# Weights times values and the output product of a masked cross-attention: float32 in 32-column tiles in place of split halves in full width

## The reference, cut to what matters

```python
q, k, v = norm(x) @ Wq.T, ctx @ Wk.T, ctx @ Wv.T       # heads of 32 columns
s = q[b, h] @ k[b, h].T / sqrt(32) + mask              # 128 x 2048
p = exp(s - max(s))
o[b, h] = (p @ v[b, h]) / sum(p)                       # 128 x 32
x[b] = x[b] + concat_h(o[b, h]) @ Wo.T                 # 128 x 512
```

## Time and profile before

| | |
|---|---|
| median of 3 runs | 1824.59 us (1823.38 to 1826.69) |
| profiled execution | 1827.8 us, its span 1826.4 us |
| TensorE, VectorE, ScalarE, GpSimd busy | 95%, 64%, 54%, 13% |
| mean granted TensorE clock | 0.983 |

### The profile page before, as it was taken

The page is one execution under the profiler, slowest core; times in us unless marked ns, Lnnn a source line. Parts: engine busy times, 40 slices in busy tenths (PEclk is TensorE's granted clock), DMA queues, the critical chain, the costliest instruction groups (busy, mean ns, idle before and its releaser), DMA issues.

```text
span 1826.4 us, 26578 instructions
## 1 busy us (share of the span) xinstructions
PE 1742.8 (95%) x9474; PEld 1429.8 (78%) x9474; DVE 1172.3 (64%) x2457; ACT 984.8 (54%) x2037; POOL 236.8 (13%) x138
## 2 busy tenths in 40 slices
PE   8999999999999999999999999999899879999998
PEld 5778888877888789999899888887455557778787
DVE  5777777765544246667677767998534356775755
ACT  6676666652443135565566656887322345665653
POOL 0000000000000031112111312232101012221222
PEclk9999999999999999999999999999999879999999
DMA  6322322217501698778677767677500347786721
GB/s 229 120 104 81 104 81 94 81 59 293 173 1 65 210 306 252 238 233 239 191 238 232 237 198 206 183 196 234 200 6 7 127 150 258 244 308 199 274 69 62
DMA packets 146848, 309.53 MB, mean 169 GB/s; under 512 B 11440, under 2 KB 100784, under 8 KB 135152
## 3 DMA queue, kind: packets, MB, share of 16 engines
q1 hardware_dynamic: 144784, 301.32, 50.9%
q0 software_dynamic: 1920, 6.36, 1.1%
HBM read 226.88 MB, written 80.76 MB: 168 GB/s over the span
## 4 chain that ended last, share of the span: by engine, by line
PE 78%; DVE 10%; ACT 4%; issue 3%; DMA 2%; DVEq 1%; SPq 1%; POOL 0%; ACTq 0%; POOLq 0%
PE bank L128 13%; PE bank L130 13%; PE bank L129 13%; PE bank L1298 4%; PE bank L2219 4%; PE bank L2220 4%; PE bank L2223 4%; PE bank L1694 4%; PE bank L1321 2%; PE bank L1322 2%; PE bank L1288 2%; DVE PTL L1428 2%; DVE TT L1417 2%; PE bank L1787 2%; ACT T L1837 1%
## 5 line engine op out<-in xcount | busy, mean ns | idle before, releaser
L1372 ACT CAST PTH<-bank 128x512 fp32r<-128x512 f32 x256 | 149.9, 586 | 166.2 <-PE bank L1298 166.2
L1428 DVE TENSOR_TENSOR PTL<-bank,PTH 128x512 fp32r<-128x512 f32 x256 | 176.0, 687 | 94.6 <-ACT PTH L1372 93.6
L2520 DVE TENSOR_TENSOR WS<-EW,WS 128x1024 fp32r<-128x1024 f32 (+1 forms) x120 | 148.3, 1243 | 83.0 <-ACT WS L2358 80.8
L1365 ACT ACTIVATE TT<-TT,MX 128x512 f32<-128x512 f32 x256 | 186.5, 729 | 8.5 <-DVE MX L1423 8.5
L1417 DVE CUSTOM_DVE_ANT_0 TT<-bank,MASK 128x512 f32<-128x512 f32 x256 | 174.2, 682 | 2.1 <-PE bank L1288 1.9
L2358 ACT CAST WS<-EW 128x1024 fp32r<-128x1024 f32 (+1 forms) x144 | 139.2, 978 | 64.5 <-PE bank L2223 63.7
L1298 PE MATMUL bank<-IDN,TT 128*128 128x128 f32 x1024 | 155.2, 274 | 4.1 <-DVE PTL L1428 3.7
L128 PE MATMUL bank<-BCH,WKT 128*128 128x256 f32 x512 | 148.2, 289 | 4.5 <-DVE BCL L355 4.5
L129 PE MATMUL bank<-BCL,WKT 128*128 128x256 f32 x512 | 144.8, 283 | 0.0
L130 PE MATMUL bank<-BCH,WKT 128*128 128x256 f32 x512 | 144.8, 283 | 0.0
L1321 PE MATMUL bank<-PTH,VG 128*128 128x256 f32 x512 | 142.6, 300 | 0.2 <-DVE PTL L1428 0.2
(11 more groups left out here) (320 smaller groups left out, 4365.3 us busy)
## 6 DMA issues: line engine op xcount, KB each, us to landing
EW<-in_ewg SPq DMA_DIRECT2D x48, 1024.0 KB, 5.6
KST<-tmp_k SPq DMA_DIRECT2D x43, 768.0 KB, 5.8
tmp_k<-EKH SPq DMA_DIRECT2D x128, 256.0 KB, 2.8
EW<-in_ewg SPq DMA_DIRECT2D x24, 768.0 KB, 4.6
CT<-in_ctxT SPq DMA_DIRECT2D x32, 512.0 KB, 3.2
CN<-in_ctxN SPq DMA_DIRECT2D x32, 512.0 KB, 3.2
BCT<-in_ctxT SPq DMA_DIRECT2D x32, 512.0 KB, 3.6
tmp_k<-EKL SPq DMA_DIRECT2D x64, 256.0 KB, 2.8
```

The lines of the kernel that those rows point to most:

```text
L1365: act.activation(TT[:, n % 4, cs], TT[:, n % 4, cs], ACT.Exp, bias=MX[:, n % 4, 5:6], scale=SC1, accum_out=SUM[:, b % 2, h, kc:kc + 1]).th ...
L1372: act.copy(PTH[:, g % NP], bank[turn_bank[g]][:]).then_inc(*p_high.up)
L1428: dve.tensor_tensor(PTL[:, q], bank[turn_bank[g]][:], f(PTH[:, q]), ALU.subtract).then_inc(*p_low.up)
```

## The change

The values stay as they are loaded, in float32, 64 columns for a pair, straight into VG; GpSimd's split is gone, and SyncE itself waits until a buffer of VG is free. The turned weights are kept in float32 in one tile PT: ScalarE copies the banks of even steps, VectorE those of odd steps. `value` now does four float32 products, each with 32 stationary columns (one head) by 128 moving ones. The two heads of a pair write 32 bank rows each, at rows 0 and 32 for even pairs, 64 and 96 for odd pairs. The reciprocals are spread by two products of the same shape, with 32 columns of ONES. OTS then has 128 distinct rows for two pairs (a "quad" of heads), the output product takes 4 tiles for a batch instead of 8, and VectorE does one multiplication for a pair instead of two. The core of the diff:

```diff
 
         WT = Region(g_at)
-        WO1 = WT("WO1", [128, 8, 512])
+        WO1 = WT("WO1", [128, 4, 512])
...
-        VG = A("VG", [128, 2, 16, 128], F32R)
+        VG = A("VG", [128, 2, 16, 64])
         at_t = A.at
-        VR = A("VR", [128, 1024])
         TT = A("TT", [128, 4, 2048])
         al = Region(at_t)
         QH = al("QH", [128, 4, 512], F32R)
         QL = al("QL", [128, 4, 512], F32R)
         NP = 4
-        PTH = A("PTH", [128, NP, 512], F32R)
-        PTL = A("PTL", [128, NP, 512], F32R)
+        PT = A("PT", [128, NP, 512])
         assert A.at <= g_at
         A = Region(wq_at)
         MASK = A("MASK", [128, 2, 2048], BF16)
         MUI = YT[:, 3, :].bitcast(I32)
         MU = YT[:, 3, :].bitcast(U8)
-        OTS = YT[:, 0:2, :].rearrange("p a (c q) -> p (a c) q", c=4)
-        LR = YT[:, 2, 0:256].rearrange("p (a q) -> p a q", a=2)
+        OTS = YT[:, 0, :].rearrange("p (c q) -> p c q", c=4)
         DG = YT[:, 2, 256:512].rearrange("p (a q) -> p a q", a=2)
         MX = A("MX", [128, 4, 8])
         SUM = A("SUM", [128, 2, 16, 4])
...
                     return None
-                if waiting[0][0] % 8 == 0 and left <= 0:
+                if waiting[0][0] % 4 == 0 and left <= 0:
                     out_bank = 2
                 if out_bank is None:
-                    if len(waiting) < 8:
+                    if len(waiting) < 4:
                         return None
-                    bk, n = 5 + turns % 2, 8
+                    bk, n = 5 + turns % 2, 4
                     turns += 1
                 else:
...
                         value_bank[v // 8] = 7 if left > 0 or v // 8 % 2 else 3
-                    if v % 8 == 7:
-                        waiting.append((v // 8, v))
+                    if v % 16 == 15:
+                        waiting.append((v // 16, v))
...
-        sums_mm, wo_mm = S.new("pe", 32), S.new("pe", 32)
-        s_exp, p_high, o_kept = S.new("act", 256), S.new("act", 256), S.new("act", 32)
+        sums_mm, wo_mm = S.new("pe", 32), S.new("pe", 16)
+        s_exp, p_act, o_kept = S.new("act", 256), S.new("act", 128), S.new("act", 32)
         cross_root = S.new("act", 3)
-        s_masked, s_max, p_low = S.new("dve", 256), S.new("dve", 64), S.new("dve", 256)
+        s_masked, s_max, p_dve = S.new("dve", 256), S.new("dve", 64), S.new("dve", 128)
         sums_diag, o_scaled, x_added, cross_var = S.new("dve", 32), S.new("dve", 32), S.new("dve", 4), S.new("dve", 3)
-        vg_high, vg_low, mask_made = S.new("pool", 32), S.new("pool", 32), S.new("pool", 4)
-        ld_qs, ld_vr, ld_mask = [S.keep("ld", 16) for _ in range(2)], S.keep("ld", 16), S.keep("ld", 16)
+        mask_made = S.new("pool", 4)
+        ld_qs, ld_vg = ([S.keep("ld", 16) for _ in range(2)] for _ in range(2))
+        ld_mask = S.keep("ld", 16)
...
+        def p_kept(g):
+
+            return (p_dve if g % 2 else p_act)[g // 2]
+
+        def rows_of(p):
+
+            return 64 * (p % 2)
+
         def cross_pe(bg, bg2):
-            emptied = {3: ev_act[31], 2: ev_dve[31]}
+            emptied = {3: ev_act[31], 2: ev_dve[31], (3, 0): ev_act[31], (3, 1): ev_act[31]}
 
             def score(g):
                 n, kc = g // 4, g % 4
@@ -1297,40 +1303,39 @@
                     kt, n = 2 * pc + j // 2, 2 * p + j % 2
                     m = pe.transpose(bank[bk][:, 128 * j:128 * j + 128], TT[:, n % 4, 128 * kt:128 * kt + 128], IDN[:])
                 m.then_inc(*t_mm.up)
-                emptied[bk] = p_low[g]
+                emptied[bk] = p_kept(g)
 
             def value(g):
                 p, pc, q = g // 8, g % 8, g % NP
-                vb = value_bank[p]
-                pe.wait_ge(*p_low[g])
+                vb, half = value_bank[p], (value_bank[p], p % 2)
+                heads = [slice(rows_of(p) + 32 * h, rows_of(p) + 32 * h + 32) for h in range(2)]
+                pe.wait_ge(*p_kept(g))
                 if pc == 0:
-                    pe.wait_ge(*vg_low[p])
-                    if vb in emptied:
-                        pe.wait_ge(*emptied[vb])
-                    emptied[vb] = o_scaled[p]
+                    pe.wait_ge(*ld_vg[p % 2][p // 2])
+                    if half in emptied:
+                        pe.wait_ge(*emptied[half])
+                    emptied[half] = o_scaled[p]
                     pe.wait_ge(*sums_diag[p])
-                    if p == 0:
-                        pe.wait_ge(*ld_lr[0])
                     for h in range(2):
-                        m = pe.matmul(bank[vb][:, 256:384], LR[:, h, :], DG[:, h, :], start=(h == 0), stop=(h == 1))
+                        m = pe.matmul(bank[vb][heads[h], 256:384], ONES[:, 0:32], DG[:, h, :], start=True, stop=True)
...
                     m.then_inc(*sums_mm.up)
                 for j in range(2):
                     kt = 2 * pc + j
-                    v = VG[:, p % 2, kt, :]
-                    js = slice(256 * j, 256 * j + 256)
-                    pe.matmul(bank[vb][:, 0:256], v, PTH[:, q, js], start=(kt == 0), stop=False)
-                    m = pe.matmul(bank[vb][:, 0:256], v, PTL[:, q, js], start=False, stop=(kt == 15))
+                    for h in range(2):
+                        at = 256 * j + 128 * h
+                        m = pe.matmul(bank[vb][heads[h], 0:128], VG[:, p % 2, kt, 32 * h:32 * h + 32],
+                                      PT[:, q, at:at + 128], start=(kt == 0), stop=(kt == 15))
                 m.then_inc(*v_mm.up)
 
             def project(step):
-                bk, pairs = step
-                if pairs[0] % 8 == 0 and bk in emptied:
+                bk, quads = step
+                if quads[0] % 4 == 0 and bk in emptied:
                     pe.wait_ge(*emptied[bk])
-                pe.wait_ge(*o_scaled[pairs[-1]])
-                for p in pairs:
-                    c = p % 8
-                    pe.matmul(bank[bk][:], OTS[:, c, :], WO1[:, c, :], start=(c == 0), stop=(c == 7)).then_inc(*wo_mm.up)
-                emptied[bk] = x_added[pairs[-1] // 8]
+                pe.wait_ge(*o_scaled[2 * quads[-1] + 1])
+                for n in quads:
+                    c = n % 4
+                    pe.matmul(bank[bk][:], OTS[:, c, :], WO1[:, c, :], start=(c == 0), stop=(c == 3)).then_inc(*wo_mm.up)
+                emptied[bk] = x_added[quads[-1] // 4]
 
             bg.rest()
             bg2(6)
...
                                accum_out=SUM[:, b % 2, h, kc:kc + 1]).then_inc(*s_exp.up)
 
             def turn(g):
-                act.wait_ge(*t_mm[g])
-                if g >= NP:
-                    act.wait_ge(*v_mm[g - NP])
-                act.copy(PTH[:, g % NP], bank[turn_bank[g]][:]).then_inc(*p_high.up)
+                if g % 2 == 0:
+                    act.wait_ge(*t_mm[g])
+                    if g >= NP:
+                        act.wait_ge(*v_mm[g - NP])
+                    act.copy(PT[:, g % NP], bank[turn_bank[g]][:]).then_inc(*p_act.up)
 
             def value(g):
                 p, pc = g // 8, g % 8
                 if pc == 7:
                     act.wait_ge(*v_mm[g])
                     if p >= 8:
-                        act.wait_ge(*wo_mm[p - 8])
-                    act.copy(OTS[:, p % 8, :], bank[value_bank[p]][:, 256:384]).then_inc(*o_kept.up)
+                        act.wait_ge(*wo_mm[(p - 8) // 2])
+                    r = slice(rows_of(p), rows_of(p) + 64)
+                    act.copy(OTS[r, p % 8 // 2, :], bank[value_bank[p]][r, 256:384]).then_inc(*o_kept.up)
 
             bg.rest()
             bg2(6)
@@ -1423,9 +1430,11 @@
                     dve.tensor_scalar(MX[:, sl, 5:6], MX[:, sl, 4:5], -SC1, None, ALU.mult).then_inc(*s_max.up)
 
             def turn(g):
-                q = g % NP
-                dve.wait_ge(*p_high[g])
-                dve.tensor_tensor(PTL[:, q], bank[turn_bank[g]][:], f(PTH[:, q]), ALU.subtract).then_inc(*p_low.up)
+                if g % 2:
+                    dve.wait_ge(*t_mm[g])
+                    if g >= NP:
+                        dve.wait_ge(*v_mm[g - NP])
+                    dve.tensor_copy(PT[:, g % NP], bank[turn_bank[g]][:]).then_inc(*p_dve.up)
 
             def pair_sums(p):
                 b, c = p // 8, 2 * (p % 8)
@@ -1441,20 +1450,16 @@
             def value(g):
                 p, pc = g // 8, g % 8
                 if pc == 7:
-                    vb, hp = value_bank[p], p % 8
+                    r, c = slice(rows_of(p), rows_of(p) + 64), p % 8 // 2
                     dve.wait_ge(*o_kept[p])
-                    for h in range(2):
-                        r = slice(64 * h, 64 * h + 64)
-                        m = dve.tensor_tensor(OTS[r, hp, :], bank[vb][r, 128 * h:128 * h + 128], OTS[r, hp, :], ALU.mult)
-                        if h == 0:
-                            own.count(m)
-                    m.then_inc(*o_scaled.up)
+                    dve.tensor_tensor(OTS[r, c, :], bank[value_bank[p]][r, 0:128], OTS[r, c, :],
```

(54 more changed lines are left out.)

## The result

The changed kernel takes 1850.62 us (median of 4 runs, 1848.71 to 1850.97), the kernel before 1825.64 beside it (4 runs). The ratio is 1.0126, 95% interval 1.0113 to 1.0138: it is slower, by 23 to 25 us, where 47 were forecast. The direction and the mechanism held; the size was near half. One of e1_order's four runs further down had a granted clock of 0.84 and took 1986.95 us: its median in the table includes that run, its ratio does not.

A forecast was written before the change was run, and what follows sets the result against it. TensorE was taken to bound the first part, VectorE and ScalarE the last 12 pairs. 40.5 + 6.5 = +47 us on 1827.8 made 1874.8, given as 1872 us for the median, range 1790 to 1905.

The forecast's parts named there:

- What bounds the kernel: Stage of the change: TensorE's own instructions set the first part (steps 0 to 159), VectorE and ScalarE the last 12 pairs.
- The value products: Each call of `value` on TensorE: 0.82 us in place of 0.48, +53.7 us over 158 calls of the first part.
- Entry: Going from full-width products into tiles on TensorE: 0.09 us more than the usual distance.
- exit: Leaving tiles on TensorE: 0.29 us from the last tiled record's start to the next full-width product.
- The 0.44: Eight value records of a call, first start to last, sharing TensorE in two tiles: 0.44 us, taken from line 1755.
- The second part: Last 12 pairs: TensorE sets the pace, 12.57 us a pair in place of 12.03, +6.5 us.
- 40.5: First part's sum in us: value products +53.7, reciprocals' products -4.6, output product -8.6.
- The smaller terms: Reciprocals' products 0.22 instead of 0.45 us, wide output product 3.45 instead of 6.91; GpSimd's split and SyncE's wait cost nothing.
- A: Rival on value products: tiles don't share TensorE but switching costs; value takes 1.15 us, time 1963 us; chance 0.17.
- C: Rival on value products: neither sharing nor switching; value takes 0.88 us, time 1894 us; chance 0.10.
- B: Rival on value products: sharing without switching cost; value takes 0.55 us, time 1803 us; chance 0.23.
- break-even: Cost of a `value` call at which the change's sign turns: 0.635 us, an overhead of 0.19 beyond the 0.44.

The follow-up runs named there:

- e1_order: Changed kernel with the four products of a value call reordered, both blocks of head 0, then both of head 1: 1856.52 us.
- e8: Changed kernel with both heads in one 64-column tile, one product by 256 moving columns for each block: 1969.67 us.
- e7: Changed kernel with values loaded twice into 128 columns and one full-width float32 product for each block, reciprocals still in tiles: 1894.61 us.
- e9: Changed kernel with both products of a block sent to head 0's 32-column tile from a pair's second step on: 1924.18 us.
- e2: Changed kernel with each value call split around the score product, two visits to the tiles for each step instead of one: 1926.82 us.
- e5: Changed kernel with the values of all eight steps of a pair in one visit to the tiles, twelve PT buffers: 1800.65 us.
- e3: Changed kernel with the values of two steps done in one visit to the tiles, eight PT buffers: 1811.84 us.
- e4: Changed kernel with the values of four steps done in one visit to the tiles, eight PT buffers: 1798.33 us.
- e12: Changed kernel with all copies of the turned banks on VectorE instead of every second one: 1853.83 us.
- e11: e4 with all copies of the turned banks on VectorE instead of every second one: 1812.98 us.
- e10: e8 with the two blocks of a call sent to different 64-column tiles, their halves not added: 1858.56 us.

## Why the prediction was wrong

**What bounds the kernel: right.** TensorE is busy for all of the 100 us from 800 on in every profile, and the sum of the changed step's pieces closes to 0.02 us.

**The value products: right mechanism, wrong size.** This is the step that failed: "value takes 0.44 + 0.29 + 0.09 = 0.82 us". Entry measured 0.10 and exit 0.31, as forecast. The 0.44 from first start to last was 0.36. I had solved the 0.44 from the 31 distances of line 1755, with groups of four in which two records of one tile follow 0.11 apart. That is not how the records of that line start, as a finer look at the kernel before shows:

```profile
1392.07 0.38 PE L1755 MATMUL bank<-KT,QT 64*128 64x128 f32 x2
...
1392.07 0.49 PE L1755 MATMUL bank<-KT,QT 64*128 64x128 f32 x4
...
1392.07 0.60 PE L1755 MATMUL bank<-KT,QT 64*128 64x128 f32 x6
...
1392.07 0.71 PE L1755 MATMUL bank<-KT,QT 64*128 64x128 f32 x8
```

They start in pairs, each pair 0.11 us after the last. Yet the wrong pattern gave the row's right number, by luck: its first eight records have 0.71 - 0.27 = 0.44 us from first start to last. What failed is that I carried this number over to the changed kernel ("columns' tiles and rows' tiles differ only in which side of the array is cut"). Three more pairs are 0.33 us in both. The difference is at the start: the first two records of line 1755 last 0.38 us, 0.11 beyond one record, those of the changed kernel 0.30, only 0.03 beyond. That 0.08 us is the 0.82 less the 0.75 measured, to 0.01.

The 0.11 is not time in which earlier products finish. Another block of line 1755, before which TensorE stood idle for 0.83 us, starts the same way:

```profile
1308.89 0.38 PE L1755 MATMUL bank<-KT,QT 64*128 64x128 f32 x2 [0.83 <-ACT KT L1826]
```

Among the blocks in tiles it goes with the columns of the stationary operand. Line 1755 loads 128 columns (a weight load of 188 ns in the median) and starts 0.11 late, e8 loads 64 (137 ns) and starts 0.43 - 0.38 = 0.05 late, the changed kernel loads 32 (110 ns) and starts 0.03 late. At full width, 128 columns start on time (e7: its first record has the usual 0.38). That the weight load is the cause is argued from these, not shown.

The step grew by 0.27 us where I had 0.34: 158 x 0.07 = 11 us of the miss.

**The second part: wrong sign, from the same term.** I had 12.57 us for a pair and it took 11.69. A call there is 0.71 us (a step of 1.38, less 0.67), 0.11 below the 0.82: 0.88 us a pair, 10.6 us for twelve. Leaving the tiles for transposes is also cheaper than leaving them for the background products: between steps at 1201.53 and 1202.91 the last tiled record starts at 1202.35 + 0.36 = 1202.71, and the transposes, recorded 0.06 longer than usual, really begin at 1202.97, 0.26 later. The lines of these two readings:

```profile
1201.53 0.66 PE L1304 MATMUL bank<-IDN,TT 128*128 128x128 f32 x4
...
1202.35 0.63 PE L1326 MATMUL bank<-PT,VG 128*32 128x128 f32 x8
1202.91 0.66 PE L1304 MATMUL bank<-IDN,TT 128*128 128x128 f32 x4
```

VectorE was no longer the limit, as forecast, though its busy time for a pair was 32.14/40 x 11.69 = 9.4 us and not 8.7, and ScalarE's 8.2 and not 7.6. Why stays open; it cost nothing here. With 11 + 10.6 us taken off and the 3 us outside the stage, 47 becomes 22.3, near the 22.9 measured. Part by part it is less close: 40.5 - 11 = 29.5 where pairs 0 to 20 measured 32.5, and 6.5 - 10.6 = -4.1 where the rest measured -6.4. These two nearly cancel; they and the 3 us outside stay open.

**The smaller terms: right.** The reciprocals' products fell from 0.45 to 0.24 us, the wide output product from 6.91 to 3.44. SyncE's wait and the value loads showed no effect, GpSimd's work on values is gone. The distance from the first value record to the first background record, for which I had 0.73, is 3.98 - 3.31 = 0.67.

**The rivals.** A (no sharing) and C are refuted by the pairs of records and by e9, which is what A would have looked like. B (no switching cost) is refuted by e2 to e5. Its break-even fits: it asked for a call of 0.635 us, and e3, with 0.75 - 0.16 = 0.59, is faster than the kernel before. In pairs of the first part only e5 is shorter than the kernel before (20.66 against 20.95 us); what e3 and e4 gain lies in the output product and in the second part.

## What to carry to other kernels

Count the changes between tiles and full width before the products in tiles. Here one visit cost 0.32 us, and the same products made the kernel 1.3% slower than the one before in 256 visits and 1.4% faster in 64 (about half of that by the shared copies). When a term is taken from a row of another shape, cut that row record by record: what its first record takes beyond the usual belongs to its own shape (here 0.11 us with 128 stationary columns, 0.03 with 32), and only the distances after it carry over. An engine relieved off the path pays only where it sets the pace, and only once the new bound has been lowered too: the halved copies were worth nothing that shows in the changed kernel (e12) and 11 to 15 us in e4 (e11, by ratios and by medians).

## What the runs showed of the hardware

- Float32 records of 128 moving columns in two 32-column tiles start in pairs, a pair every 0.11 us; all in one tile, one every 0.11 us (e9). With 256 moving columns in 64-column tiles it is 0.21 to 0.22 us, for a pair in two tiles (e10) and for a single record in one (e8). The tiles read the same 128 rows.
- The order of a call's products didn't matter to this (e1 against the changed kernel), though they are issued one head after the other.
- Score products with 96 rows, between full-width transposes and background products, cost no visit (0.31 us from their start to the next full-width product's, before and after).
